# Products of one token tile as items of their own, new orders on every engine, and PSUM banks given out from a list within each chain

## What is computed

```
x = x + layernorm(attention(layernorm(x)))      # 16 heads, causal, latent k/v, shared rope
x = x + layernorm(ffn0(layernorm(x)))           # 256 -> 1024, relu squared, ternary weights
x = x + layernorm(mixer(layernorm(x)))          # z = x@W_in, short conv, p = exp(..), cos/sin of k*theta,
                                                # running sums of p*cos and p*sin over tokens, query, silu, W_out
x = x + layernorm(ffn1(layernorm(x)))           # 256 -> 1024, relu, 1024 -> 256 with biases
```

## Time and profile before

| what | value |
|---|---|
| median of three runs | 1407.12 us |
| span of the profiled execution | 1405.9 us |
| what lies between the two | 1.2 us |
| instructions | 23146 |
| mean granted TensorE clock | 0.936 of full |

### The profile page before, as it was taken

The page is one execution under the profiler, slowest core; times in us unless marked ns, Lnnn a source line. Parts: engine busy times, 40 slices in busy tenths (PEclk is TensorE's granted clock), DMA queues, the critical chain, the costliest instruction groups (busy, mean ns, idle before and its releaser), DMA issues.

```text
span 1405.9 us, 23146 instructions
## 1 busy us (share of the span) xinstructions
PE 1216.6 (87%) x8060; PEld 778.2 (55%) x8060; DVE 1089.1 (77%) x2259; ACT 1052.2 (75%) x2103; POOL 333.9 (24%) x317
## 2 busy tenths in 40 slices
PE   5889885999899988998799989999899988977347
PEld 2575653465556754675556755666566655534224
DVE  3683388788788979889788989898688988887830
ACT  4675788797959878797859888788949887458522
POOL 3944110520133102320124112310133110510101
PEclk9799996999999999999999999999999999998669
DMA  8504141514142123521333041523151140031100
GB/s 254 113 9 102 27 130 42 115 31 116 46 102 72 23 75 88 126 46 41 98 91 82 24 128 28 132 44 103 38 120 38 26 131 28 23 96 50 37 0 15
DMA packets 72084, 101.65 MB, mean 72 GB/s; under 512 B 10640, under 2 KB 44064, under 8 KB 71968
## 3 DMA queue, kind: packets, MB, share of 16 engines
q1 hardware_dynamic: 71968, 100.16, 27.3%
HBM read 74.44 MB, written 25.69 MB: 71 GB/s over the span
## 4 chain that ended last, share of the span: by engine, by line
PE 54%; DVE 16%; ACT 16%; issue 6%; POOL 5%; SPq 1%; DMA 1%; POOLq 0%; DVEq 0%; ACTq 0%
PE ps L873 19%; PE ps L883 15%; PE ps L956 5%; DVE work L1516 4%; ACT work L1203 4%; PE ps L1042 4%; DVE work L1439 3%; PE ps L974 3%; PE ps L948 3%; ACT work L1210 3%; DVE work L1507 2%; ACT xnd L1146 2%; DVE work L1525 2%; PE ps L865 1%; DVE work L1394 1%
## 5 line engine op out<-in xcount | busy, mean ns | idle before, releaser
L1516 DVE TENSOR_TENSOR_SCAN work<-work 128x512 f32<-128x512 f32 x256 | 313.1, 1255 | 39.5 <-ACT work L1270 37.8
L1203 ACT ACTIVATE work<-work 128x384 f32<-128x384 f32 (+3 forms) x512 | 264.4, 559 | 54.6 <-DVE work L1439 52.7
L1439 DVE CUSTOM_DVE_ANT_0 work<-ps,work 128x384 f32<-128x384 f32 (+3 forms) x512 | 228.0, 486 | 90.8 <-PE ps L948 87.0
L752 POOL TENSOR_TENSOR later_norms<-later_norms,singles 128x2 f32<-128x2 f32 x112 | 97.0, 867 | 768.9 <-ACT xnd L1146 465.4
L956 PE MATMUL ps<-ident,work 128*128 128x128 f32 x1280 | 203.4, 285 | 21.4 <-DVE work L1439 10.2
L956 PEld LDWEIGHTS ps<-ident,work 128*128 128x128 f32 x1280 | 151.8, 145 | 84.5 <-issue 35.3
L1210 ACT COPY work<-ps 128x512 f32<-128x512 f32 x300 | 169.9, 573 | 7.8 <-PE ps L956 7.3
L1525 DVE TENSOR_TENSOR work<-work 128x1024 f32<-128x1024 f32 x128 | 160.0, 1250 | 4.3
L948 PE MATMUL ps<-work 96*128 96x384 bf16 (+3 forms) x512 | 124.1, 310 | 38.7 <-ACT work L1210 32.1
L873 PE MATMUL ps<-led_xTd,wf 128*128 128x512 f32 x256 | 120.3, 621 | 3.9 <-issue 3.9
L873 PE MATMUL ps<-led_xTd,wfc 128*128 128x512 f32 x256 | 118.0, 596 | 0.0
(11 more groups left out here) (176 smaller groups left out, 1950.7 us busy)
## 6 DMA issues: line engine op xcount, KB each, us to landing
work<-values SPq DMA_DIRECT2D x64, 256.0 KB, 3.1
work<-ratios SPq DMA_DIRECT2D x64, 256.0 KB, 3.2
scratch<-work SPq DMA_DIRECT2D x32, 384.0 KB, 4.7
work<-scratch SPq DMA_DIRECT2D x64, 192.0 KB, 3.9
work<-scratch SPq DMA_DIRECT2D x64, 128.0 KB, 4.2
x_in<-x SPq DMA_DIRECT2D x8, 512.0 KB, 6.7
work<-scratch SPq DMA_DIRECT2D x64, 64.0 KB, 4.3
values<-work SPq DMA_DIRECT2D x16, 256.0 KB, 3.2
```

Source lines behind the costliest of these rows:

```text
L1203: i = s_.activation(part_of, part_of, ACT.Exp, scale=-1.0, bias=nmax[:, row:row + 1])
L1439: i = v_.tensor_tensor_reduce(sc[:, n % 4, at:at + nk], out_of(b, name)[:, at:at + nk], base_of(qt), -SCORE_SCALE, BIG, ALU.add, ALU.min, ...
L1516: v_.tensor_tensor_scan(ring[:, at, m, :], pwr[:, slot, :], ring[:, at, m, :], 0.0, ALU.mult, ALU.add).then_inc(*scanned.one)
```

## The change

`tokens_out` becomes `token_out`: one token tile is an item. out, oout, fproj and gproj have four items in place of one or two, so PE's table may put other work between any two of them; the matmuls are the same ones, and the bank is still reported as filled after the second tile of a half. PE has 1304 items where it had 1224; the other engines have as many as before.

All five tables of `MERGE` are new. `plan_banks` no longer deals banks by turns: a string `BANKS` lists, in PE's own order, the bank of each product, and PV and the gathers take part in it. After batch 0 chain a still uses banks 0 to 2 (and 3 for PV), chain d 4 to 6 and chain m 7, but which of the three a product takes is free. The copy of PV's bank now counts as its drain, in place of a semaphore of its own.

```diff
-            def tokens_out(b, tag, half, lhs, rhs, n_k):
-                name = f"{tag}{half}"
-                may_fill(pe, b, name)
-                for t in range(2):
-                    tt = 2 * half + t
-                    for j in range(n_k):
-                        i = mm(ps[:, bank(b, name), t * D:(t + 1) * D], lhs[:, j, tt * P:(tt + 1) * P],
-                               rhs[:, j, :], start=j == 0, stop=j == n_k - 1)
-                i.then_inc(*fills(b, name))
+            def token_out(b, tag, tt, lhs, rhs, n_k):
+                name = f"{tag}{tt // 2}"
+                if tt % 2 == 0:
+                    may_fill(pe, b, name)
+                for j in range(n_k):
+                    i = mm(ps[:, bank(b, name), tt % 2 * D:(tt % 2 + 1) * D], lhs[:, j, tt * P:(tt + 1) * P],
+                           rhs[:, j, :], start=j == 0, stop=j == n_k - 1)
+                if tt % 2:
+                    i.then_inc(*fills(b, name))
...
+def token_items(item, half):
+    return [(item, 2 * half), (item, 2 * half + 1)]
...
+    place, uses, fills, banks = {}, [0] * 8, [0] * 8, iter("".join(BANKS.split()))
+    for chain, b, item, n in order_of("pe"):
+        for name in names_of(item, n) if chain != "p" else ():
+            k = int(next(banks))
+            uses[k] += 1
+            fills[k] += item not in ("PV", "gather")
+            place[b, name] = (k, uses[k], fills[k])
...
                     if k == 0:
-                        need(pe, o_copied, b, hg)
+                        may_fill(pe, b, f"PV{hg}")
...
 MERGE = {
     "pe":
-        "a5 p a3 p a6 p4 a34 p a24 p a31 p3 a6 p a p a p a p a p a5 d a2 d a2 d a4 d6 a3 d a6 d a3 d a6 d a12 "
+        "a8 p a2 p3 a4 p2 a41 p2 a2 p a15 p a24 p a2 p a2 p a3 p a p a5 p a14 d a2 d a4 d6 a2 d a d a7 d a3 d a d "
...
+BANKS = """
+0124501245012540125401254012403514025401240514205421305214052145201524052134021542015204120542013540
```

More of the change, by code:

```diff
@@ L234, in merged @@
     return order
+def merged(engine):
+    return order_of(engine)
 def turn_on_act(b):
     return b in (0, B - 1)
[L241 to L274 removed]
@@ new lines, in names_of @@
+def names_of(item, n):
+    if item in ("xT", "attnT"):
+        return [item + "0", item + "1"]
+    if item in ("out", "fproj", "oout", "gproj", "gather"):
+        return [f"{item}{n // 2}"] * (n % 2 == 0)
+    if item == "PV":
+        return [f"PV{n // len(SUMS)}"] * (n % len(SUMS) == 0)
+    if item in ("ckv", "qr", "kr", "total"):
+        return [item]
+    if item in ("q", "k", "v", "base", "S", "T", "OT", "fxT", "fc", "zxT", "z", "query", "gxT", "gc"):
+        return [f"{item}{n}"]
+    return []
@@ L277 @@
+def plan_banks():
+    place, uses, fills, banks = {}, [0] * 8, [0] * 8, iter("".join(BANKS.split()))
[5 more added lines that the diff above has]
+            place[b, name] = (k, uses[k], fills[k])
+    assert next(banks, None) is None
+    return place, uses, fills
 class Signal:
@@ L440, in sandwich_kernel @@
         ps = ctx.enter_context(nc.psum_tensor("ps", [P, 8, 512], F32))
[L441 to L445 removed]
+        filled = [signal(f"bank{k}_filled", 0, 1, n) for k, n in enumerate(bank_fills)]
+        drained = [signal(f"bank{k}_drained", 0, 1, n) for k, n in enumerate(bank_uses)]
         x_loaded = signal("x_loaded", 1, 16)
@@ L1030, in do @@
                 if item == "query":
-                    product(b, f"q_{n}", out_of(b, f"q_{n}"),
+                    product(b, f"query{n}", out_of(b, f"query{n}"),
                             [(wqc[:, n // MH, c, n % MH, :], xd_c[c]) for c in range(DC)])
```

123 lines of the change are left out of this document (51 added, 72 removed), and 89 rows, old and new, of the table MERGE.

## The result

The changed kernel takes 1443.4 us in the median of four runs, beside 1408.0 for the kernel before on the same chip: a ratio of 1.0262, 95% interval 1.0237 to 1.0287. (One execution of the kernel before took 1527.1 us; it is in that median and left out of the ratio.) The change is slower, and lies outside the forecast range.

A forecast was written before the change was run, and what follows sets the result against it. PE was taken to bound the middle (260 to 1144 us), with waits for DMA, ACT and DVE limiting other stages. Terms +4.7 - 1.9 - 3.5 - 3 - 7 = -10.7 took 1405.9 to 1395.2, 1396.4 as median; range 1385 to 1408.

The forecast's parts named there:

- Start: Before S 0: ternary 0 ahead of the statistics on DVE delays S 0, +4.7 us, bounds +2 and +5.8.
- End of the first attention: Three of prep 12 to 15 move into batch 0's attention, two thirds of 5.7 us returning as delay: -1.9.
- The hole: 210 to 260 us: exp 37 comes earlier on ACT, shortening PE's wait before S 39: -3.5, bounds -11.7 and +2.3.
- The middle: 260 to 1144 us, PE full: free banks, products in halves and table loads together give -3 us.
- Free banks: Middle: a bank that DVE empties can replace S's waits for ACT's copies, 11.3 us: -6, bounds -11.3 and 0.
- Table loads: Middle: 20 more loads, 25.7 us of ACT work, mostly hidden because PE rarely waits for ACT: +3, bounds 0 and +25.7.
- Products in halves: Middle: attention units wait behind 16 matmuls, not 32; DVE waits for that but isn't the bound: 0, bounds -3 and +2.
- The tail: Last mixer: shorter ACT path to the first cos, scans begin 6.5 us earlier: -7, bounds -14 and 0.
- R1: 260 to 1144 us: half of PE's 56.4 us idle time closes, -28 in place of -3, 1371.4; chance 0.24.
- R2: First half of each attention: ACT becomes the bound, all 25.7 us of loads reach PE, 1419.1; chance 0.17.
- R3: Each switch costs ACT twice, standing empty beside each load: 20 x 1.28 = 25.7 more, 1444.8; chance 0.03.
- R4: Hole and last mixer: no gains, since DVE and not ACT ends these waits, 1409.9; chance 0.08.

The follow-up runs named there:

- ternary_first: Kernel before with ternary 0 put ahead of the statistics on DVE, nothing else changed: 1410.1 us, ratio 1.0038.
- prep_new: Kernel before with PE, ACT and DVE in the changed kernel's order for what they began from 60 to 111 us: 1414.1 us, ratio 1.0059.
- before_free: Kernel before, orders kept, each product of batches 1 to 7 given the bank of its chain that its profile shows emptied first: 1406.6 us, ratio 1.0011.
- after_noswitch: Changed kernel, same order, eleven groups of lone sin and cos waves made with the exponential, 20 table loads fewer: 1441.9 us, ratio 1.0262.
- before_loads: Kernel before's orders in the changed code, ten one-element sines put ahead of exps in batches 2 to 7, 20 table loads more: 1438.2 us, ratio 1.0235.
- after_halves: Changed kernel with the two token tiles of each half product side by side on PE, in 22 places: 1476.6 us, ratio 1.0501.
- tail1145: Kernel before's order for what began before 1145 us, changed kernel's order for the rest: 1398.5 us, ratio 0.9951.
- tail1255: Kernel before's order for what began before 1255 us, changed kernel's order for the rest (around the last mixer): 1399.8 us, ratio 0.9958.
- second_head: Kernel before with PE, ACT and DVE in the changed kernel's order for what they began from 246 to 310 us: 1414.5 us, ratio 1.0063.

## Why the prediction was wrong, and where it was right

*Start, on record +4.7.* Right: ternary_first gave 5.5, and S 0 came 4.25 later in the changed kernel.

*End of the first attention, -1.9.* Wrong in sign: prep_new gave +8.7, outside the bounds of -5.7 to +1. The step let the work go into "the 5.7 us that are free there" in the attention of batch 0. These pieces of idle time were not free: the marks show the attention's end 10 us later in that run's trace and only 3 of it back before batch 1. In the changed kernel the first products of batch 1 came 9.9 later, where about 3 was forecast. The step also left out DVE's `tables`, which moved into the same attention; PE's wait behind them (2.37) is one part of the loss, and how the rest divides was not tried.

*The hole, -3.5.* Half right. What the step said of S 39 came true, and from S 30 of batch 1 to the first product of batch 2 the changed kernel is 5.8 us quicker (by the marks, 50.7 before and 44.9 after). It lost 4.4 of that in the ten scores from S 10 on. Put into the kernel before, the order of the stretch cost 9.8. The term was a part of a stretch, taken for the whole. (There is a slip in it as well: a load and a sin of 1.28 + 1.0 leave 1.1 of 3.4 us, not 1.4.)

*The middle, -3.* Here the prediction failed; the change lost 43 there. Its rule for this stage, "an instruction moved within the full middle costs or wins little", was wrong: mid_new, in which nothing but the middle's order and banks changes, is 42.6 slower. Three prices stood in the step, and the one that decided was not among them.
- "Free banks -6": 0 in before_free. PE's short waits for ACT's copies did not go when the banks were changed.
- "Table loads +3": 0 in the new order (after_noswitch), but 33 in the old one. The reasoning, "a us of ACT work costs PE about 0.05", from waits of 34.6 us beside 724 of ACT work, is wrong: in before_loads a us cost 1.2. A small sum of waits for an engine doesn't say that there is slack behind it. In before_loads the scores' waits for ACT's copies (line 964 there) rose from 11.3 us to 26.1, and PE was busy 11.2 us longer besides:

```profile
PE ps L964 <- ACT work L1226: 26.1, 28, 2.8
```

- "Products in halves: ... PE does not wait for that, DVE does, and DVE isn't the bound: 0". This is the sentence that failed, in its reason more than in its subject: the cuts are not the loss (after_halves), but DVE was taken to have slack, and all that moved on it was put at nothing. The step priced what was added and never read DVE's new order in the middle, where every scan and mix stands elsewhere than before. PE's 11 us of waits for a DVE that is busy 753 of 884 us were taken as slack too; they became 37.6, and halving the scans and mixes of six batches gave back 31 us, where it gives 9 in the kernel before.

*The tail, -7.* Right: -7.6 in tail1145, -5.6 in tail1255, with the scans 8.5 earlier where 6.5 was forecast. The lower bound of -14 was too wide: it lets the last gather save 3.4 of the 3.41 us that it takes, while an equal gather of that trace, at 1291.86, took 1.92.

*The rivals.* R1 (idle time closes) did not come. R2 gave the side and a third of the loss, but by ACT, which after_noswitch excludes: PE's waits for ACT are 38.7 where R2 asked for over 55. R3 gave 1444.8, within 2 us of the result, for a reason that isn't there: a load takes 1.28 us and the cos behind it starts 0.02 us later (1308.07 and 1309.37 in the tail's rows above), and without 20 of them the time is the same. That its number came out is luck. The Trainium skill (ScalarE: Activation LUTs, section "What ACT_TABLE_LOAD costs") puts some 2.66 us on a switch; before_loads, the run in which switches are paid in full, lost 1.67 for each of its 20, the ten sines within it, and there too a load follows the instruction before it without a gap (0.3 and 0.2 us of idle time in all before the 24 and the 10 loads in the rows above). R4 was about hole and tail, and both moved.

Of the signs named in the prediction PE's share of the middle fell under 92 per cent, as R2 has it, while its waits for ACT did not grow: no rival stood for an engine other than ACT. That DVE's mixer work moves in front of the attention's head could have been read from the orders of the two kernels, row by row.

## What to carry to other kernels

Where engines with fixed orders depend on one another all the time, a wait that is short in the profile is no measure of slack: put a known amount of dummy work in (here 27.7 us on ACT, 33 us of time) or take a known amount out (half of each scan, 9 us in one order, 31 in the other) and read the price. When a change gives every engine a new order, compare for each engine what now stands ahead of the instruction that feeds the critical engine, in particular at the head of a stage, and not only what the diff adds; most of a delay there stays (8.7 us of 13.4 at the last score in second_head). And try a new order stretch by stretch: the tail of this one was worth 0.5 per cent by itself while its middle cost 3.

## What the runs showed of the hardware that was not expected

DVE's scans and mixes get longer beside POOL's work. In the head of batch 2 in second_head a pair of scans took 3.97 us and a mix 1.88, while a mix at 274.89 and the scans at 297.75 took 1.22 and 2.33. POOL, in the same stretch, squares relu outputs; in this trace the 34 of them with no scan, mix or other TENSOR_TENSOR out of SBUF on DVE beside them take 1.10 in the mean, and the four beside the long rows take 7.54, 1.89 each. POOL's timeline there with a pair of DVE's scans, and the stage view of the first long pair and of the short one:

```profile
278.02 1.10 POOL L786 TENSOR_TENSOR hid<-hid 128x512 f32<-128x512 f32 x1 [0.34 <-ACT hid L1237]
278.14 3.17 DVE L1528 TENSOR_TENSOR_SCAN work<-work 128x512 f32<-128x512 f32 x2
...
284.31 7.54 POOL L786 TENSOR_TENSOR hid<-hid 128x512 f32<-128x512 f32 x4 [0.18 <-ACT hid L1237]
```
```profile
283.10:287.10 4.00, 4.00 (x10) 1.71 (x10) 4.00 (x3) 3.83 (x6) 3.82 (x3) 1.00 0.50 101
...
297.70:300.10 2.40, 2.40 (x9) 2.02 (x8) 2.40 (x4) 0.00 (x0) 0.00 (x0) 0.68 0.00 0
```

Over the whole changed kernel the mean scan is 1285 ns and the mean mix 1301, against 1255 and 1250 before, 256 and 128 of them: 321.4 and 166.6 us in place of 313.1 and 160.0, some 15 of DVE's 20.6 added us.

```profile
L1530 DVE TENSOR_TENSOR_SCAN work<-work 128x512 f32<-128x512 f32 x256 | 321.4, 1285 | 48.8 <-ACT work L1284 46.8 <-DVE x L1373 1.7
...
L1539 DVE TENSOR_TENSOR work<-work 128x1024 f32<-128x1024 f32 x128 | 166.6, 1301 | 5.2 <-DVE x L1373 0.2
```

The Trainium skill (SBUF — State Buffer, section "Who interferes with whom") says that a DVE instruction with two inputs in SBUF contends with a GpSimd instruction that reads SBUF, and calls the ports that they share an exclusive lock, where the order of issue decides which of the two is held. The trace agrees as to the first: scans and mixes have two such inputs, and in second_head none of those without a POOL instruction beside it took over 1.23 us. One place fits the second: the square at 278.02 began ahead of the scans at 278.14 and took its 1.10, while that pair of scans took 3.17. In the long rows, where both are longer, the two are not told apart. That the order puts the mixer beside POOL's squares is a part of its price, but how much of the 43 us this makes was not tried by itself.
